# Attention's small VectorE operations rewritten: reduces instead of two-input joins, pieces cut in PSUM, Newton steps on GpSimd

## The reference, cut to what matters

```python
qkv = x @ qkv_w.T                         # 16 heads of 16 channels, rotary on q and k
heads 0..5:   softmax(q k^T / 4, causal) v
heads 6..9:   arg = max(curv*(tq*tk - q k^T), 1+1e-7)        # hyperbolic heads
              dis = sqrt(1/curv) * arccosh(arg)
              softmax(1/(1e-6 + dis), causal) v
heads 10..15: the same softmax on normalised q, k, scale 4
x = layernorm(x + (y @ proj_w.T + proj_b))                   # first normalisation
x = layernorm(x + experts(x))             # 1024 rows through 8 experts, top 2
```

## Time and profile before

| | before |
|---|---|
| median of 3 runs | 2314.19 us (2304.13 to 2318.62) |
| profiled execution, its own time | 2313.54 us |
| its span | 2312.0 us |
| mean granted TensorE clock | 0.898 of full speed |
| PE / DVE / ACT / POOL busy | 78% / 62% / 62% / 30% |

### The profile page before, as it was taken

The page is one execution under the profiler, slowest core; times in us unless marked ns, Lnnn a source line. Parts: engine busy times, 40 slices in busy tenths (PEclk is TensorE's granted clock), DMA queues, the critical chain, the costliest instruction groups (busy, mean ns, idle before and its releaser), DMA issues. The chain is left out here.

```text
span 2312.0 us, 39981 instructions
## 1 busy us (share of the span) xinstructions
PE 1806.9 (78%) x13330; PEld 965.2 (42%) x13330; DVE 1422.5 (62%) x3280; ACT 1422.3 (62%) x1400; POOL 683.8 (30%) x332
## 2 busy tenths in 40 slices
PE   6888888843887896897797787888789689746994
PEld 3434443421333443343344343444434334325893
DVE  4767676772663776676676777776777667650113
ACT  1333333321887888788788888788788878811110
POOL 0000000001443534444444444543444365510002
PEclk9999999975997998998998999999899899878997
DMA  5222333328026006207306304504502620119972
GB/s 190 85 103 109 110 110 110 110 107 166 1 45 96 11 16 125 66 1 122 83 2 113 92 2 84 121 2 70 126 11 31 137 55 23 42 51 350 345 276 66
DMA packets 88461, 217.50 MB, mean 94 GB/s; under 512 B 14112, under 2 KB 34848, under 8 KB 83936
## 3 DMA queue, kind: packets, MB, share of 16 engines
q1 hardware_dynamic: 79840, 184.74, 30.5%
q0 software_dynamic: 8448, 30.41, 4.2%
HBM read 146.52 MB, written 68.58 MB: 93 GB/s over the span
## 5 line engine op out<-in xcount | busy, mean ns | idle before, releaser
L1067 ACT ACTIVATE a_PT<-a_s 128x1024 f32<-128x1024 f32 (+3 forms) x576 | 461.3, 808 | 206.8 <-PE a_s L889 135.0
L886 PE MATMUL a_s<-a_Q,a_K 96*128 96x512 bf16 (+7 forms) x1152 | 331.3, 350 | 157.0 <-ACT a_PT L1067 108.7
L1245 DVE TENSOR_REDUCE a_mx<-a_w 128x1 f32<-128x512 f32 (+2 forms) x576 | 305.9, 550 | 53.0 <-PE a_w L917 36.8
L1145 POOL TENSOR_TENSOR a_Z<-a_Z,a_R 128x2182 f32<-128x2182 f32 x64 | 290.4, 4537 | 94.0 <-ACT a_R L1079 94.0
L1142 POOL TENSOR_TENSOR a_R<-a_Z 128x2182 f32<-128x2182 f32 x64 | 244.6, 3822 | 217.2 <-DVE a_Z L1237 130.7
L245 PE MATMUL p_ps<-p_xT,p_w 128*128 128x512 f32 x512 | 248.0, 645 | 46.4 <-ACT p_xT L341 25.5
L901 PE MATMUL a_o<-a_PT,a_V 128*32 128x512 f32 (+3 forms) x2304 | 276.0, 554 | 6.4 <-ACT a_PT L1067 6.4
L1237 DVE TENSOR_SCALAR_CACHE_REDUCE a_Z<-a_w 128x512 f32<-128x512 f32 (+7 forms) x384 | 202.0, 530 | 120.2 <-PE a_w L929 85.3
L946 PE MATMUL a_w<-a_ident,a_R 128*128 128x128 f32 (+1 forms) x1152 | 207.4, 306 | 75.2 <-DVE a_PTh L1294 63.9
L1294 DVE COPY a_PTh<-a_w 128x512 f32<-128x512 f32 (+1 forms) x256 | 156.4, 618 | 141.0 <-PE a_w L946 138.8
L886 PEld LDWEIGHTS a_s<-a_Q,a_K 99*128 99x128 bf16 (+1 forms) x1152 | 111.0, 102 | 250.5 <-ACT a_PT L1067 140.6
(11 more groups left out here) (161 smaller groups left out, 2961.9 us busy)
## 6 DMA issues: line engine op xcount, KB each, us to landing
e_w<-in_w SPq DMA_DIRECT2D x23, 2048.0 KB, 8.5
qk_parts<-p_parts SPq DMA_DIRECT2D x32, 768.0 KB, 3.5
a_Q<-qk_parts SPq DMA_DIRECT2D x144, 128.0 KB, 4.7
a_K<-qk_parts SPq DMA_DIRECT2D x144, 128.0 KB, 6.6
v_rows<-p_vt SPq DMA_DIRECT2D x8, 2048.0 KB, 7.7
a_V<-v_rows SPq DMA_DIRECT2D x32, 512.0 KB, 8.1
p_xin<-in_x SPq DMA_DIRECT2D x8, 1024.0 KB, 6.7
a_X<-in_x POOLq DMA_DIRECT2D x8, 1024.0 KB, 11.3
```

The costliest lines, as they stand in the source:

```text
L886: m = pe.matmul(sB[x % 2][:, i, 0:w], Kb[0:r, h, P * j:P * j + P], Qb[0:r, h, t0:t0 + w], start=True, stop=not diag)
L1067: act.activation(PT[:, u % 2, 2 * k:2 * k + 2, 0:w], sB[x % 2][:, :, 0:w], ACT.Exp, scale=scale_of(GROUPS[g][2 * k])).then_inc(prob.sem, 1)
L1145: pool.tensor_tensor(z, z, r, ALU.add).then_inc(z_sum.sem, 1)
L1245: dve.tensor_reduce(mx[:, pc, col:col + 1], wB[x % WB][:, 0:w], AX.X, ALU.max).then_inc(wide_free.sem, 1)
```

## The change

1. `join_maxima` becomes one `tensor_reduce` with `max` over the two pieces, negated, into a new tile `mneg`; the separate negation goes.
2. `row_bias` becomes two `tensor_reduce` of 2 and 2 columns, negated, straight into `nb`, with no wait between them.
3. `cut_maxima` no longer copies the transposed maxima to SBUF first: the parts are cut from the PSUM bank and the rest is written back into the same bank, columns 128 to 255. The bank is freed after the last cut and not after the first copy.
4. The four Newton operations move from VectorE to GpSimd as an item `newton` with a wait after each.
5. `normalize` is two items of four row tiles each, and all late items get new slots. Before, the numbers were 108, 111, 113 (normalize 0), 115 (mid_out), 119 (add_bias), 121 and 123 (statistics), 125 (variance 1), 127 (inverse_root 1), 129 (normalize 1), 132 (rows_out), 143 (rows_in).
6. In the tail the two transfers out are items of their own places in the list; GpSimd issued them in the same order before.

```diff
-        work[27][0].append(("variance", 0))
-        work[27][3].append(("inverse_root", 0))
-        work[28][1].append(("normalize", 0))
-        work[28][3].append(("mid_out",))
-        work[29][3].append(("add_bias",))
-        work[30][1].append(("statistics", 1, 0, NT // 2))
-        work[30][3].append(("statistics", 1, NT // 2, NT))
-        work[31][1].append(("variance", 1))
-        work[31][3].append(("inverse_root", 1))
-        work[32][1].append(("normalize", 1))
-        work[33][0].append(("rows_out",))
-        work[35][3].append(("rows_in",))
+        for at, item in ((108, ("variance", 0)), (111, ("inverse_root", 0)), (115, ("newton", 0)), (117, ("normalize", 0, 0)),
+                         (118, ("normalize", 0, 1)), (119, ("mid_out",)), (123, ("add_bias",)),
+                         (125, ("statistics", 1, 0, NT // 2)), (127, ("statistics", 1, NT // 2, NT)), (129, ("variance", 1)),
+                         (130, ("inverse_root", 1)), (132, ("newton", 1)), (134, ("normalize", 1, 0)),
+                         (135, ("normalize", 1, 1)), (136, ("rows_out",)), (143, ("rows_in",))):
+            put(at, item)
...
-                    pe.transpose(bank[0:c1 - c0, 0:P], mx[:, 0, c0:c1], ident[:]).then_inc(wide_full.sem, 1 + MORE * r)
+                    pe.transpose(bank[0:c1 - c0, 0:P], mneg[:, c0:c1], ident[:]).then_inc(wide_full.sem, 1 + MORE * r)
...
+                elif kind == "newton":
+
+                    pool.wait_ge(rs_exp.sem, rs_exp.at(d, n))
+
+                    def step(k, ins):
+                        ins.then_inc(rs_step.sem, 1)
+                        pool.wait_ge(rs_step.sem, rs_step.at(d, 4 * n + k))
+
+                    step(0, pool.tensor_tensor(rs[:, 2], rs[:, 0], rs[:, 1], ALU.mult))
+                    step(1, pool.tensor_tensor(rs[:, 2], rs[:, 2], rs[:, 1], ALU.mult))
+                    pool.sem_inc(pool_passed, 1)
+                    step(2, pool.tensor_scalar(rs[:, 2], rs[:, 2], -0.5, 1.5, ALU.mult, ALU.add))
+                    step(3, pool.tensor_tensor(rs[:, 1], rs[:, 1], rs[:, 2], ALU.mult))
+                    pool.sem_inc(pool_passed, 1)
...
-                dve.tensor_tensor(mx[:, 0, c0:c1], mx[:, 0, c0:c1], mx[:, 1, c0:c1], ALU.max).then_inc(m_step.sem, 1)
-                dve.wait_ge(m_step.sem, m_step.at(b, 6 * r))
-                dve.tensor_scalar(mx[:, 0, c0:c1], mx[:, 0, c0:c1], -1.0, None, ALU.mult).then_inc(m_step.sem, 1)
+                dve.tensor_reduce(mneg[:, c0:c1], mx[:, :, c0:c1].rearrange("p k c -> p c k"), AX.X, ALU.max, negate=True) \
+                    .then_inc(m_step.sem, 1)
...
-                row, rest, part = mrow[0:c1 - c0, 0, :], mrow[0:c1 - c0, 1, :], mpart[0:c1 - c0, r]
+                bank, part = wB[x % WB][0:c1 - c0], mpart[0:c1 - c0, r]
+                row, rest = bank[:, 0:P], bank[:, P:2 * P]
...
-                dve.tensor_copy(row, wB[x % WB][0:c1 - c0, 0:P]).then_inc(wide_free.sem, 1 + MORE * r)
-                dve.wait_ge(wide_free.sem, wide_free.at(b, x + MORE * r))
...
+                dve.wait_ge(m_step.sem, m_step.at(b, 5 * r + 4))
+                dve.sem_inc(wide_free.sem, 1 + MORE * r)
...
-                dve.tensor_tensor(r[:, UW + 2:UW + 4], r[:, UW:UW + 2], r[:, UW + 2:UW + 4], ALU.max).then_inc(b_max.sem, 1)
-                dve.wait_ge(b_max.sem, b_max.at(d, n))
-                dve.tensor_scalar(nb[:, n % 2, :], r[:, UW + 2:UW + 6], -1.0, None, ALU.mult).then_inc(b_ready.sem, 1)
+                dve.tensor_reduce(nb[:, n % 2, 0:2], r[:, UW:UW + 4].rearrange("p (c s) -> p s c", s=2), AX.X, ALU.max, negate=True)
+                dve.tensor_reduce(nb[:, n % 2, 2:4], r[:, UW + 4:UW + 6].unsqueeze(2), AX.X, ALU.max, negate=True) \
+                    .then_inc(b_ready.sem, 1)
...
-                    step(0, dve.tensor_tensor(rs[:, 2], rs[:, 0], rs[:, 1], ALU.mult))
-                    step(1, dve.tensor_tensor(rs[:, 2], rs[:, 2], rs[:, 1], ALU.mult))
-                    step(2, dve.tensor_scalar(rs[:, 2], rs[:, 2], -0.5, 1.5, ALU.mult, ALU.add))
-                    step(3, dve.tensor_tensor(rs[:, 1], rs[:, 1], rs[:, 2], ALU.mult))
-                    for n in range(NT):
+                    _, a, part = item
+                    if part == 0:
+                        dve.wait_ge(rs_step.sem, rs_step.at(d, 4 * a + 3))
+                    for n in range(NT // 2 * part, NT // 2 * (part + 1)):
                         ins = dve.tensor_scalar(X[:, n, :], X[:, n, :], mv[:, n, 0:1], rs[:, 1, n:n + 1],
                                                 ALU.subtract, ALU.mult)
-                    ins.then_inc(normed.sem, 1)
+                    if part:
+                        ins.then_inc(normed.sem, 1)
```

More of the change, by code:

```diff
@@ L714, in attend @@
         last_argument = [item for item in ringed if item[0] == "argument"][-1]
-        LATE = ("turn_rows", "project", "statistics", "variance", "inverse_root", "normalize", "add_bias", "mid_out", "rows_out", "shift")
+        LATE = ("turn_rows", "project", "statistics", "variance", "inverse_root", "newton", "normalize", "add_bias", "mid_out",
+                "rows_out", "shift")
         def is_late(item):
@@ L725, in attend @@
             tail += [("turn_rows", n + 1)] * (n + 1 < NT) + [("project", n), ("statistics", 0, n, n + 1)]
-        tail += [("variance", 0), ("inverse_root", 0), ("normalize", 0), ("add_bias",), ("statistics", 1, 0, NT),
-                 ("variance", 1), ("inverse_root", 1), ("normalize", 1)]
+        tail += [("variance", 0), ("inverse_root", 0), ("newton", 0), ("normalize", 0, 0), ("normalize", 0, 1), ("mid_out",),
+                 ("add_bias",), ("statistics", 1, 0, NT), ("variance", 1), ("inverse_root", 1), ("newton", 1),
+                 ("normalize", 1, 0), ("normalize", 1, 1), ("rows_out",)]
         tail_wide = {item: x for x, item in enumerate([it for it in tail if it[0] in RINGED])}
@@ L765, in attend @@
         M_ROWS = 4 * NT
-        mrow = sb("a_mrow", [M_ROWS, 2, P])
+        mneg = sb("a_mneg", [P, N_DOT * NT])
         mpart = sb("a_mpart", [M_ROWS, 2, 3, P], BF16)
@@ L800, in attend @@
         wide_full, wide_free = ev("a_wide_full", n_wide, carried=True), ev("a_wide_free", n_wide, carried=True)
-        m_step = ev("a_m_step", 12)
+        m_step = ev("a_m_step", 10)
         z_sq = ev("a_z_sq", NU)
@@ L806, in attend @@
         d_inv = ev("a_d_inv", NU, carried=True)
-        b_max, b_ready = ev("a_b_max", NU), ev("a_b_ready", NU)
+        b_ready = ev("a_b_ready", NU)
         h_prob, h_masked = ev("a_h_prob", 4 * NU), ev("a_h_masked", 2 * NU)
@@ L861, in _ @@
                     c0, c1 = columns_of(r)
-                    sp.wait_ge(m_step.sem, m_step.at(b, 6 * r + 5))
+                    sp.wait_ge(m_step.sem, m_step.at(b, 5 * r + 4))
                     sp.dma_start(m_parts[c0:c1], mpart[0:c1 - c0, r]).then_inc(m_sent.sem, 16)
@@ L1006, in do @@
                     c0, c1 = columns_of(r)
-                    pe.wait_ge(m_step.sem, m_step.at(b, 6 * r + 1))
-                    pe.transpose(bank[0:c1 - c0, 0:P], mx[:, 0, c0:c1], ident[:]).then_inc(wide_full.sem, 1 + MORE * r)
+                    pe.wait_ge(m_step.sem, m_step.at(b, 5 * r))
+                    pe.transpose(bank[0:c1 - c0, 0:P], mneg[:, c0:c1], ident[:]).then_inc(wide_full.sem, 1 + MORE * r)
                 elif kind == "turn":
@@ L1196, in _ @@
                 do(B, B - 1, item)
-            rows_out(B - 1, x_mid, 0, mid_sent)
-            rows_out(B - 1, io["out"], 1, out_sent)
             pool.wait_ge(spread_out, 16 * NCOL)
@@ L1357, in do @@
                 elif kind == "normalize":
-                    a = item[1]
-                    dve.wait_ge(rs_exp.sem, rs_exp.at(d, a))
-                    def step(k, ins):
-                        ins.then_inc(rs_step.sem, 1)
-                        dve.wait_ge(rs_step.sem, rs_step.at(d, 4 * a + k))
-                    step(0, dve.tensor_tensor(rs[:, 2], rs[:, 0], rs[:, 1], ALU.mult))
-                    step(1, dve.tensor_tensor(rs[:, 2], rs[:, 2], rs[:, 1], ALU.mult))
-                    step(2, dve.tensor_scalar(rs[:, 2], rs[:, 2], -0.5, 1.5, ALU.mult, ALU.add))
-                    step(3, dve.tensor_tensor(rs[:, 1], rs[:, 1], rs[:, 2], ALU.mult))
-                    for n in range(NT):
+                    _, a, part = item
+                    if part == 0:
+                        dve.wait_ge(rs_step.sem, rs_step.at(d, 4 * a + 3))
+                    for n in range(NT // 2 * part, NT // 2 * (part + 1)):
                         ins = dve.tensor_scalar(X[:, n, :], X[:, n, :], mv[:, n, 0:1], rs[:, 1, n:n + 1],
                                                 ALU.subtract, ALU.mult)
-                    ins.then_inc(normed.sem, 1)
+                    if part:
+                        ins.then_inc(normed.sem, 1)
                 elif kind == "add_bias":
```

8 lines of the change are left out of this document (3 added, 5 removed).

## The result

The changed kernel takes **2328.36 us** (median of 14 runs, 2321.05 to 2337.72), the kernel before 2307.46 us beside it: ratio **1.0095**, 95% interval 1.008 to 1.0109. That is slower by just under 1%, where 2292 us was forecast in a range of 2268 to 2314.

A forecast was written before the change was run, and what follows sets the result against it. No engine is full; TensorE and ScalarE hand work back and forth and stall when blocked VectorE keeps them waiting. 7 x (1.4 + 0.5) + 8 x 1.3 - 2 = 21.7 us off 2313.54 gave 2292 us, range 2268 to 2314.

The forecast's parts named there:

- I take 5.9: landing at 1087.2.: Normalisation 0: the x_mid transfer, issued at about 1081.3, lands after the median 5.9 us, so VectorE's add_bias waits 3 us.
- the second rival: x_mid lands after add_root starts, so add_bias is blocked behind it; slower, 2337 us; chance 0.12.
- A: Normalisation 0, 7 sequences: the ring goes on, but a moved block and later x_mid take part back; net gain 1.4 us.
- B: Normalisation 1, 7 sequences: nothing blocks normalize any more; gain 0.5 us, between 0 and 3.2.
- Its point of decision: Normalisation 0: if x_mid lands later than 7.6 us after its issue, add_bias waits for add_root until 1093.6.
- C: Join of round 1, 8 sequences: tensor_reduce takes 0.2 us beside GpSimd; gain 1.3 us, between 0.66 and 3.6.
- A's gross gain: Normalisation 0: without the stop, ScalarE reaches the exponential begun at 1086.40 at 1082.5; 3.9 us before losses.
- The block of `normalize` 0: Normalisation 0: normalize now waits behind GpSimd's square until 0.2 us before its end, 1078.5, and ends at 1081.2.
- fewer such stretches: Sign to look for: fewer stretches of TensorE at 1.2 GHz behind normalisation 0.
- The rest: Parts cut in PSUM 0, at worst 1 us each; row_bias 0; Newton on GpSimd about 1.5 us, hidden in the loop.
- the +1 us each of the sum: Tail: nothing hides Newton on GpSimd, where four VectorE operations took 0.8 us; +1 us twice, +2 us.
- The first rival: All of A's gross gain comes through, normalisation not blocked or transfer early enough; 2274 us; chance 0.24.

The follow-up runs named there:

- e11: Changed kernel with one SyncE wait moved, so the next sequence's Q and K loads begin about 1.5 us after the x_mid transfer is issued: ratio 0.9989.
- e1: Kernel before with only the joins and row maxima by tensor_reduce and the parts of the maxima made in PSUM: ratio 0.9928.
- e9: e4 with the slots of e2 up to the x_mid transfer, add_bias left at slot 123: ratio 0.9818.
- e4: Changed kernel with a second tile for the rows from add_bias on, so add_bias does not wait for the x_mid transfer: ratio 0.9834.
- e12: e9 with the statistics and variance of normalisation 1 one slot earlier and its root one slot later: ratio 0.9813.
- e10: e1 with the second tile of e4, Newton on VectorE and the old slots: ratio 0.9888.
- e2: Changed kernel with Newton 0, normalize 0 and the x_mid transfer at earlier slots, ahead of square of unit 7: ratio 1.0112.
- e5: e2 with the next sequence's Q and K loads begun behind the transposed sums of slot 121, after the x_mid transfer is issued: ratio 0.9888.
- e7: Slots of e2 with the second tile of e4, add_bias at slot 117, statistics and normalisation 1 three to six slots earlier: ratio 0.9968.
- e3: Changed kernel without the add_bias operation, its wait for the x_mid transfer kept: ratio 0.9994.
- e6: Changed kernel with add_bias three slots later (126, not 123) and what follows one or two slots later: ratio 1.0042.
- e8: Kernel before with only Newton on GpSimd, the new slots and the new tail; joins and maxima as before: ratio 1.0198.

## Why the prediction was wrong

**The step that failed: "I take 5.9: landing at 1087.2."** The block moved to the normalisation as forecast (blocked behind `square`, transfer issued late). The landing decides between a small gain and a loss, and its time was taken from a row in which `x_mid` stood ahead of the loads of Q and K. The prediction's own steps put it behind them: it has the last `argument` item earlier and the transfer later, and SyncE's loads hang on that item. It named the loads under the second rival and gave them no price. Measured: 7.0 to 8.7 us in the six sequences with loads. e11 shows it: with that one order restored 5.9 us comes back, all eight `add_bias` are short, and 24 of the 44 us between forecast (0.9906) and result (1.0095) are gone. The other 20 are terms that were mis-sized: the half with Newton and the new slots was put 25 us too high even with the landing right, and the joins' half 6 us too low.

**So it was the second rival.** Its mechanism and its price for A hold: by its working a sequence's part A is -5.0 us, and the table has +4.6 - 9.4 = -4.8 from 49 to 64. That its sum agrees as well, +23 us forecast and +21 measured (medians), is luck in part. Per sequence it has B as a gain of 0.5, where the table loses 1.0 from 64 to 73; it has the join at 1.3, where the table has 2.5; and it counts seven such sequences, where there are six. Its point of decision, 7.6 us from issue to landing, was put almost a microsecond too late: `add_root` starts 6.7 to 6.95 us behind the issue, so that even the quickest landing of the six (7.03 us) was behind it. The forecast's 5.9 us would still have been in time. The rival's chance of 0.12 was too low. Its cause lay in rows that could be read before: which queue starts first.

**The other terms.**
- C, the joins: 1.3 us for each of 8 forecast, 10 us; 16 us measured for the whole half (e1). The price of the reduction (0.2, measured 0.19) was right. The table has 2.5 us per sequence there, the transpose's stop of 1.65 and more, so the value lay between the forecast and its upper bound of 3.6.
- A's gross gain: 3.9 forecast, 4.6 in the table. Its net at a landing after 5.9 us: 1.4 forecast, 0.6 in e11 from 49 to 64. `add_bias` waits 4.2 us there, not 3, and ScalarE stands 3.6 to 4.0 us, not 2.5.
- The block of `normalize` 0: forecast until 0.2 us before the end of `square`, and so it came (3.59 us, ending 0.15 us behind it, as forecast for an operation of 0.4 us). The row that it was read from could not show it, though. The 634 ns began with the mask, not behind it, and the longest `tensor_scalar` of the earlier trace rows, 762 ns at 2017.70, was under way before the mask began, beside nothing of GpSimd but the issue of an indirect transfer. The row is of the kernel before:

```profile
2017.37 1.01 POOL L1170 DMA_INDIRECT xs<-a_first,r_pos  x1 [0.32 <-issue]
```

- B, normalisation 1: of a gain of 0.5 nothing is left, and 1.3 us are lost from 64 to 67 in after and in e9, 2.0 in e11. In e4, e9 and e12, where VectorE does not wait for the transfer, the root is asked for before VectorE has the variance, and ScalarE waits 1.1 us for it in each of seven sequences. In after and e11 it does not wait there at all; it stands for scores, 1.10 and 0.18 us in one sequence of after, 1.47 and 0.72 in one of e11. Why these scores come late is not settled.
- The start of a sequence: 1.5 to 2.6 us are lost by exponential 5 in each kernel of the table with the new slots and not in e1, with TensorE at 1.2 GHz; at exponential 40 they stand 0.7 to 1.9 us behind e1. The forecast had fewer such stretches and looked only behind normalisation 0. Which of the moved steps puts the stretch there is not settled. What TensorE did before it differs, as read ahead of the fifth sequence: in before its last stop of over a microsecond is 3.2 us for VectorE, 7.7 us ahead of the start; in after it stops 1.2 and 2.1 us for ScalarE, 6.4 and 4.0 us ahead of it.
- The rest as forecast: Newton's operations 0.2 us each, the parts in PSUM nothing. In the tail VectorE waits 1.76 us for `newton` twice, where its own four operations took 0.8: the +1 us each of the sum.
- The first rival's 29 us for Newton's move were too high: 16 us by the ratios where VectorE does not wait (e9 over e10).
- What is left once the landing is put right: e11 stands 14 us above e1, where 7 x 1.9 - 2 = 11 us below were forecast. The table has e11 3.2 us per sequence above e1 in place of 1.9 below. Of these 5.1 us the start up to exponential 40 has 1.9, A 1.0 and B 2.5, and 0.3 come back elsewhere. Seven times that is more than the 25 us of the ratios; the profiled execution of e11 is the slowest of its twelve runs.

## What to carry to other kernels

When an edit lets one engine run earlier, ask what it sets off on other queues, and whether a transfer that someone waits for now stands behind them: the order of issue was worth 24 us here, with no instruction changed. A landing time taken from a trace holds only for the transfers that stood around it. Earlier slots alone gained nothing (e2), and with the loads moved behind the transfer as well the kernel is 48 us under the changed one (e5). And where an operation in place waits for its tile to be written out, a second tile removes wait and block together, here for 60 us with no new slot and no other order of transfers (e4).

## What the runs showed of the hardware

- The block goes both ways, and the later one waits. `add_bias` behind `add_root` ends 2.1 us after it, nearly its whole 2.29 us; `add_root` behind `add_bias` takes 5.98 to 6.34 us and not 4.8, in 6 of e11's sequences. That is what the Trainium skill, SBUF — State Buffer, "Who interferes with whom", says: the order of issue decides which of the two is blocked.
- In e7 `add_bias` begins 0.56 us before `square` by the record and is held all the same: 6.56 us, its own 2.29 and `square`'s 3.84. GpSimd had begun to issue the transfer 0.4 us before it, and `square` shows no lengthening. Whether the issue of the transfer counts as the earlier operation here, no run separates.
- `tensor_scalar` with pointers to its scalars, SBUF to SBUF, is blocked as well (3.6 us in six sequences, 3.9 in the seventh, 0.41 in the median). `tensor_reduce` is not: 202 to 206 ns in the 8 joins that run beside `square`, where the two-input join took 3.7 to 3.8 us. The Trainium skill, same page and section, has both: `tensor_scalar` can contend with GpSimd, `tensor_reduce` never does on trn2.
- The same 1 MB to DRAM landed after 5.9 us where it was issued 1.7 to 2.1 us ahead of SyncE's loads, after 10.7 us where it was issued 4.3 us behind their start (e2), and after 7.5 to 8.6 us where it was issued some 7.9 us behind it (the medians of after, e3, e4, e6 and e8).
